# Attention stage of a two-layer kernel: three projection products ahead of each unit's transposes, no longer behind them

## What is computed

```
x1 = LayerNorm(x + gelu(x @ w1 + b1) @ w2 + b2)    # or a small 4-wire circuit model, by a flag
h  = LayerNorm(x1) * (1 + scale) + shift
q, k, v = h @ Wq, h @ Wk, h @ Wv                    # 16 heads of 32 channels
p  = softmax(q k^T / sqrt(32) + attention_bias, masked)
x2 = h + (p @ v) @ Wo + bo
out = x2 + gelu2(LayerNorm(x2) @ W1 + b1) @ W2 + b2
```

## Time and profile before

| | us |
|---|---|
| median of 3 runs | 2472.27 (2470.9 to 2473.67) |
| the profiled execution's own time | 2467.16 |
| its span, first to last instruction | 2465.4 |
| TensorE matmul busy | 2378.8 (96%) |
| VectorE busy | 1353.1 (55%) |
| ScalarE busy | 1009.6 (41%) |
| GpSimd busy | 1015.0 (41%) |

### The profile page before, as it was taken

The page is one execution under the profiler, slowest core; times in us unless marked ns, Lnnn a source line. Parts: engine busy times, 40 slices in busy tenths (PEclk is TensorE's granted clock), DMA queues, the critical chain, the costliest instruction groups (busy, mean ns, idle before and its releaser), DMA issues. The chain is left out here.

```text
span 2465.4 us, 44348 instructions
## 1 busy us (share of the span) xinstructions
PE 2378.8 (96%) x16068; PEld 1900.1 (77%) x16068; DVE 1353.1 (55%) x2749; ACT 1009.6 (41%) x2057; POOL 1015.0 (41%) x829
## 2 busy tenths in 40 slices
PE   5999999999999899999999999998999999999999
PEld 4688888888887677777777777776788888888887
DVE  5355545544546777777776677778553333333322
ACT  4231331322333676766676666666431111211111
POOL 0032422422424696766676667659022022112210
PEclk9999999999999999999999999999999999999999
DMA  5201101101113456555555555565420110110100
GB/s 160 91 18 60 43 17 60 43 17 60 43 62 126 129 185 193 168 188 179 180 183 173 164 178 177 172 189 180 133 70 16 51 51 0 51 51 0 51 35 18
DMA packets 133617, 244.21 MB, mean 99 GB/s; under 512 B 13212, under 2 KB 17452, under 8 KB 133440
## 3 DMA queue, kind: packets, MB, share of 16 engines
q1 hardware_dynamic: 133440, 241.92, 30.8%
HBM read 216.69 MB, written 25.20 MB: 98 GB/s over the span
## 5 line engine op out<-in xcount | busy, mean ns | idle before, releaser
L1137 POOL TENSOR_TENSOR at_bias<-at_bias,at_mask 128x512 f32<-128x512 f32 x512 | 591.6, 1182 | 252.3 <-DMA at_bias<-in_fside_Bx16xSxS 232.0
L597 ACT ACTIVATE L_hid<-bank,L_b1c 128x512 f32<-128x512 f32 x256 | 176.6, 690 | 969.8 <-PE bank L290 965.1
L765 DVE CAST L_hh<-L_hid 128x512 fp32r<-128x512 f32 x256 | 123.8, 484 | 761.5 <-PE bank L873 723.8
L288 PE MATMUL bank<-xth,L_w1h 128*128 128x512 f32 x1024 | 403.4, 394 | 5.9 <-ACT L_hid L597 5.1
L871 PE MATMUL bank<-L_w2h,L_hh 128*128 128x512 f32 x1024 | 401.4, 392 | 0.0
L289 PE MATMUL bank<-xth,L_w1l 128*128 128x512 f32 x1024 | 400.0, 391 | 0.0
L290 PE MATMUL bank<-xtl,L_w1h 128*128 128x512 f32 x1024 | 400.0, 391 | 0.0
L873 PE MATMUL bank<-L_w2l,L_hh 128*128 128x512 f32 x1024 | 398.7, 389 | 0.0
L872 PE MATMUL bank<-L_w2h,L_hl 128*128 128x512 f32 x1024 | 398.6, 389 | 0.0
L1193 ACT ACTIVATE at_bias<-at_bias,cos_sin 128x512 f32<-128x512 f32 x512 | 363.2, 713 | 9.9 <-DVE cos_sin L1330 9.9
L1330 DVE CUSTOM_DVE_ANT_0 at_bias<-bank,at_bias 128x512 f32<-128x512 f32 x512 | 333.5, 684 | 51.8 <-PE bank L1516 31.5
(11 more groups left out here) (185 smaller groups left out, 3221.0 us busy)
## 6 DMA issues: line engine op xcount, KB each, us to landing
at_bias<-in_fside_Bx16xSxS SPq DMA_DIRECT2D x256, 512.0 KB, 3.7
L_xin<-in_x SPq DMA_DIRECT2D x8, 1024.0 KB, 5.4
L_xres<-in_x SPq DMA_DIRECT2D x8, 1024.0 KB, 5.4
x_scratch<-L_xres SPq DMA_DIRECT2D x8, 1024.0 KB, 4.3
at_xin<-x_scratch SPq DMA_DIRECT2D x8, 1024.0 KB, 6.1
at_xres<-x_scratch SPq DMA_DIRECT2D x8, 1024.0 KB, 7.0
L_xin<-x_scratch SPq DMA_DIRECT2D x8, 1024.0 KB, 5.7
L_xres<-x_scratch SPq DMA_DIRECT2D x8, 1024.0 KB, 5.5
```

The lines of the kernel that those rows point to most:

```text
L288: nc_mm = pe.matmul(out, ah, bh, start=i == 0, stop=False)
L597: nc.scalar.activation(hid[m % 2][:, :], turn[m % 2][:, :], func, bias=b1c[:, m:m + 1]).then_inc(h_act, 1)
L1137: nc.gpsimd.tensor_tensor(tile, tile, mask[:, m % TT, :], ALU.add).then_inc(masked, 1)
```

## The change

In the loop over the four units, the call of `beside` and the call of `turn_unit` change places:

```
                     elif m == 9 and j < 2:
                         pe.wait_ge(xt_lo, x_count(b + 1) + 3 + j)
+                    beside(b, m, j, first, last)
                     turn_unit(b, m, j, first)
-                    beside(b, m, j, first, last)
                 if m % TT == TT - 1:
                     over(b, m // TT)
```

## The result

The changed kernel takes 2527.38 us (median of 4 runs, 2525.44 to 2529.35), the kernel before in the same session 2472.97 us. The ratio is 1.0217, with a 95% interval of 1.0201 to 1.0232: slower by 54 us.

A forecast was written before the change was run, and what follows sets the result against it. TensorE's list bounds the kernel; the change acts through its waits. Middle batches 42.7, first 3.9, last 5.0 make 51.6 us; with 3 for the clock, 2467.16 becomes 2521.8, and 5.1 to the median gives 2527 us, range 2503 to 2548.

The forecast's parts named there:

- Part 2: Wait of a slot's first product for bank gen: chain from unit 2's transposes 4.04 us against 3.57, 0.54 in slots 6, 7, 11.
- The rival in which the bank is free in time: ScalarE and VectorE return gen within 3.57 us of unit 2's transposes, so all stops vanish: 2470 us, chance 0.04.
- a start from standstill: After a wait for gen, the product following the first comes somewhat later: 0.07 us added to the 0.47 stop.
- Part 3: Slot 3: TensorE waits for the output tile, which VectorE reaches late behind unit 1's transposes: 1.66 us.
- Part 4: What is late next: bias loads and mask on transposes 0.7 later in a slot, 0; clock falls, 3 us.
- Part 1: Same TensorE work in another order within a slot: 0, range -3 to +11 us for 110 slots with projections.
- The knock-on rival: Context waits for unit 3's copy, 0.12 us over in each of 110 slots, 13 us: 2540 us, chance 0.17.
- growth of slots 2 and 14: Sign in slot lengths: 2 and 14 stay at 6.57 us by the forecast; if they grow, the knock-on is right.
- One or two more falls: Granted clock, seen in slots 8 and 9: one or two further drops at 2.4 us each, 3 us.
- The rival in which the clock follows each short stop: Clock falls at each of the 60 new stops, 2.4 us each, another 144 us: 2670 us, chance 0.03.
- the smaller stops: Releases 0.2 us quicker than in the one stopped case and slot 3 half, 25 us remain: 2498 us, chance 0.08.

## Why the prediction was right

**The bound.** TensorE bounds the stage, and the change was to act only through its waits. That is so for 42.2 of the 62.1 us. The other 19.9 are busy time, for which the prediction had 0 (the order) and 3 (the clock). Of them 2.0 us a middle batch stand where the granted clock is 1.00 (109.9 us before and 111.9 now over the 16 slots of the table); a part of these is the modelled end of the matmul before each stop.

**Part 2, the chain for gen.** The chain was forecast at 4.04 and measured at 4.05. Moving the high part took these waits away with TensorE's list untouched, so the cause is shown, not only argued. The rival in which the bank is free in time fails on the same numbers. The sizes agree less well than the slots do:

- Slots 6 and 11 got 0.54 and show 0.55. But the stop is 0.44, where 0.47 and 0.07 for a start from standstill had been put, and the other 0.11 is the cost of the order, which was to be nothing. Behind a stop three products take 0.80 us (1361.55 to 1362.35), as they do behind the context without a stop (1345.77 to 1346.57), so no run shows the 0.07.
- Slots 1 and 5 got 0.78 as a wait for the bank and show 0.87 and 0.86. In slot 1 the larger part is the context's wait for unit 3's copy (0.54 against 0.25 for the bank), in slot 5 it is 0.32 against 0.49. The size was right and the cause half right, which is luck.
- Slots 0 and 12 got 0.61 and show 0.57 and 0.60.
- The waits for `at_nat` come to 21.6 us in 49, not to 30 in 60. In slots 0 behind the loop's jump and in slot 8 there is none.

**Part 3, slot 3.** 1.66 forecast, 1.81 measured. The terms as written give 1.89 for the stop, not 1.86, and the trace has 1.88: from the transposes' start to the tile 2.67 (1338.62 to 1341.29), less 0.79 for two blocks of transposes (1350.13 to 1350.92 where units 2 and 3 are in the old order). From it goes what stood before, 0.15 and not 0.2 (the same blocks took 0.94, 1299.87 to 1300.81), and the cost of the order comes on top.

**Slots 7 and 8, an omission and a misread term.** Slot 7 cost 1.21 instead of 0.54: the wait of `turn_x` for unit 3's copy was missing from the sum, and Part 4, which asks what is late next, does not name it. Unit 3 alone in the new order isolates it. Slot 8 cost nothing instead of 0.43. The low part there was to be 0.4 later than 1.40 behind the slot's start, but in batch 3 (slot 8 from 1254.40) it is not later:

```profile
1255.75 0.74 DVE L1318 SCALAR_TENSOR_TENSOR at_nat<-bank,at_biases,at_nat 128x512 fp32r<-128x512 f32 x1
```

That is 1.35. My reading, not tested apart, is that slot 8 begins 0.67 us later than in the forecast, and ScalarE and VectorE, which bound it, use that time to catch up. The two errors cancel to 0.2 us a batch.

**Part 1, taken as 0.** It is 0.04 to 0.12 a slot, some 8 us in all, within the bounds. The step from transposes to scores costs the 0.18 that was forecast, and 0.16 of it comes back as forecast. On top come 0.04 from scores to context and 0.03 for the first three products (0.80 against 0.77). The rule of the Trainium skill, "TensorE: Matmul & The Clock Gate", The mechanism, that weight loads overlap matmuls only in other row groups, would have put its cost between context and projection; there the trace has 1.01 us, as it had before transposes, so nothing is added to this step.

**The knock-on rival.** By the prediction's own sign, growth of slots 2 and 14 means that this rival is right. They grew by 0.11, about its price of 0.12 a slot, but only 0.04 of it is at the context; the sign could not tell the two apart. In slots 1, 5 and 13, behind `context_lo`, the context does wait, 0.54, 0.32 and 0.31 longer than before. The prediction had this for slot 13 alone (0.24).

**The clock.** One or two more falls were put at 3 us. Slots 8 and 9, where most of them happen, answer in batches 3 and 4 to the earlier trace rows:

```profile
1254.40:1262.63 8.23, 5.86 (x73) 4.27 (x72) 6.90 (x16) 6.65 (x15) 5.19 (x5) 1.00 0.52 145
1262.63:1269.90 7.27, 6.67 (x74) 5.17 (x74) 4.46 (x11) 3.62 (x8) 3.95 (x4) 1.00 0.68 217
1374.88:1383.56 8.68, 6.20 (x73) 4.45 (x72) 7.43 (x16) 6.64 (x15) 5.62 (x5) 0.96 0.55 157
1383.56:1391.53 7.97, 7.86 (x74) 5.93 (x74) 4.03 (x11) 3.63 (x8) 3.49 (x4) 0.83 0.56 181
```

Batch 4 takes 16.65 us in these two slots with the lower clock (17.43 before), batch 3 15.50 (15.06 before). Over the compared stretch the two traces have 34 and 48 us at 1.2 GHz. At the price of batch 4 before (2.4 us for 6.8 us at that level) the difference is an estimated 5 us of the 62. Half of it is in one slot behind the loop's jump, slot 0 of batch 3, which took 9.16 us at 0.70 and 6.57 before at 1.00.

The rival in which the clock follows each short stop is refuted: slots 1, 5, 6, 7 and 11 of the six middle batches have a stop each, and none of the stretches at 1.2 GHz lies in them. In slot 5 of the first batch one does, behind two longer stops:

```profile
858.46 1.08 PE L1533 MATMUL bank<-at_pt,at_v 128*32 128x128 f32 x32 [1.19 <-issue]
860.37 0.64 PE L1463 MATMUL bank<-xth,at_wqh 128*128 128x512 f32 x1 [0.83 <-DVE at_nat L1318]
```

That slot took 10.39 us, against 7.63 before and 8.78 in the changed kernel with slot 3 in the old order, where the clock did not fall in it.

**The sum.** Forecast 54.6 us over the profiled execution, measured 62.2. The middle batches took 7.5 us more than their 42.7 and the first batch 3.4 more than its 3.9, most of that in the slot 5 just named; the last took 0.4 less, and the 3 us for the clock are inside these. The median came out at 2527.38 against 2527, but that closeness is luck: the offset of 5.1 us between profiled execution and median that I added was -2.0 us in the changed kernel. The lower end of the range, 2503, stands above the 2498 of the smaller stops that it was to take in.

## What to carry to other kernels

When work is moved ahead of a step, look at who starts from that step: here the products moved by 0.4 us relative to their own wait, but the emptying of their bank is queued behind copies that start from the transposes, and these moved by 0.7 us the other way. A single buffer with 0.6 us of slack cannot take both. Count every wait between the moved step and the end of its slot, and list each engine's order from the first late item on, since an engine with idle time on average may have none in the stretch that counts. And compare busy time between the same two instructions of both kernels, not between rough ends of a stage: here a third of the loss was busy time.

## What was not expected

ScalarE, busy for 613.66 of the 967.73 us compared, is without a gap for 3.9 us of a 7.42 us slot once unit 0 is late. One 0.7 us operation per slot, moved on it, cost 10 us in the kernel before, nearly all through slots 8 and 9: slot 8 alone isn't bounded by TensorE, and the clock in slot 9 behind it was lower. Slots 8 and 9 in which the clock fell differ from run to run of near-equal programs by up to 2 us, so savings of under 5 us were readable only slot by slot. The clock explains little of the 54 us between the medians: the four executions of the changed kernel had mean granted clocks of 0.987 to 0.989, those of the kernel before beside the experiments 0.985 to 0.989.
